# A mixture-of-experts block on one core: one-hots of seven batches made ahead by GpSimd, a ring of seven, logits copied by ScalarE

## The reference

```python
def _L0_ffn_ref(hidden_states, gate_w, Wg, Wu, Wd, Ws_g, Ws_u, Ws_d):
    b, s, d = hidden_states.shape            # 32, 256, 128
    e = gate_w.shape[0]                      # 16 experts
    cap = int(s * 2.0 / e)                   # 32 rows of each batch for each expert
    logits = jnp.einsum('bsd,ed->bse', hidden_states, gate_w)
    scores = jax.nn.softmax(logits, axis=-1).transpose(0, 2, 1)
    topk_w, topk_idx = jax.lax.top_k(scores, cap)
    x_tok = jnp.take_along_axis(hidden_states[:, None, :, :], topk_idx[..., None], axis=2)
    g = jnp.einsum('becd,efd->becf', x_tok, Wg)
    u = jnp.einsum('becd,efd->becf', x_tok, Wu)
    h = jax.nn.gelu(g, approximate=False) * u
    eo = jnp.einsum('becf,edf->becd', h, Wd) * topk_w[..., None]
    ...
    flat = flat.at[flat_idx].add(eo.reshape(-1, d))
    ...
    shared = jnp.einsum('bsf,df->bsd', jax.nn.gelu(gs, approximate=False) * us, Ws_d)
    return out + shared
x = L0_attn_x
x = x + _layernorm(_L0_attn_ref(_layernorm(x), ...))
x = x + _layernorm(_L0_ffn_ref(_layernorm(x), ...))
```

## Time and profile before

| | |
|---|---|
| median of 3 runs | 1394.62 us |
| lowest and highest | 1392.88 and 1401.41 us |
| profiled execution | 1400.59 us |
| its span, first to last instruction | 1398.9 us |
| TensorE busy | 1094.9 us, 78% of the span |
| VectorE busy | 1103.3 us, 79% |
| ScalarE busy | 889.4 us, 64% |
| GpSimd busy | 938.9 us, 67% |

### The profile page before, as it was taken

One profiled execution on the slowest core, in us unless ns is written; L12 is line 12 of the kernel. 1 busy time (PEld: TensorE's weight loads), 2 busy tenths in 40 slices (PEclk: granted clock), 3 DMA queues, 4 the chain that ended last, 5 costly groups with the idle time before them and its releaser, 6 DMA issues. The chain is left out here.

```text
span 1398.9 us, 15385 instructions
## 1 busy us (share of the span) xinstructions
PE 1094.9 (78%) x4128; PEld 510.1 (36%) x4128; DVE 1103.3 (79%) x1440; ACT 889.4 (64%) x1614; POOL 938.9 (67%) x503
## 2 busy tenths in 40 slices
PE   4667878787777878777777876445998989999796
PEld 2322222222222222222222322133755336666695
DVE  7499999999999999999999999896382962222288
ACT  3567577667667677667667665356332866666796
POOL 0199999999999999999999999722010740000176
PEclk9878899989999899989998898867798999999898
DMA  5745835834834835834834836110000001111013
GB/s 159 152 101 112 183 71 111 182 81 101 182 77 105 182 75 107 182 85 97 182 81 101 183 81 162 41 31 1 1 0 23 1 1 34 44 35 34 12 31 91
DMA packets 48490, 122.87 MB, mean 88 GB/s; under 512 B 5824, under 2 KB 20928, under 8 KB 42304
## 3 DMA queue, kind: packets, MB, share of 16 engines
q1 hardware_dynamic: 46864, 121.01, 39.1%
q10 hardware_dynamic: 1584, 1.36, 0.3%
HBM read 83.55 MB, written 5.24 MB: 63 GB/s over the span
## 5 line engine op out<-in xcount | busy, mean ns | idle before, releaser
L555 POOL TENSOR_TENSOR states<-b_dup,dup 128x1024 f32<-128x1024 f32 x256 | 596.5, 2359 | 63.3 <-DMA dup<-dd 61.7
L648 DVE TENSOR_TENSOR_SCAN da<-da,states 128x1024 f32<-128x1024 f32 x160 | 359.5, 2283 | 38.7 <-ACT da L397 32.6
L397 ACT ACTIVATE da<-dup,decay 128x510 f32<-128x510 f32 x512 | 327.2, 672 | 11.1 <-DVE states L648 11.1
L295 PE MATMUL yp<-states,fold 128*64 128x512 f32 x1024 | 275.4, 664 | 15.6 <-DVE states L574 9.8
L534 POOL TENSOR_TENSOR states<-states,X 128x1024 f32<-128x1024 f32 x96 | 226.1, 2356 | 20.5 <-DVE states L648 20.4
L648 DVE TENSOR_TENSOR_SCAN states<-da,states 128x1024 f32<-128x1024 f32 x96 | 218.7, 2278 | 7.0 <-ACT da L397 7.0
L574 DVE TENSOR_TENSOR states<-da,X 128x1024 f32<-128x1024 f32 x160 | 192.5, 1203 | 0.0
L1664 POOL TENSOR_SCALAR put<-row_t,slot_i,slot_w 128x256 f32<-128x256 f32 x32 | 39.1, 1222 | 193.3 <-POOLq L1368 173.5
L393 ACT ACTIVATE da<-zeros 128x4 f32<-128x4 f32 x177 | 30.5, 173 | 197.2 <-DVE states L574 196.3
L295 PEld LDWEIGHTS yp<-states,fold 128*64 128x64 f32 x1024 | 69.4, 152 | 212.5 <-issue 196.2
L1469 DVE TENSOR_TENSOR hx<-glx,upx 128x512 f32<-128x512 f32 x64 | 41.3, 684 | 126.6 <-ACT glx L1434 118.2
(11 more groups left out here) (185 smaller groups left out, 1779.9 us busy)
## 6 DMA issues: line engine op xcount, KB each, us to landing
b_dup<-bc_rows SPq DMA_DIRECT2D x32, 1024.0 KB, 9.6
dup<-dd SPq DMA_DIRECT2D x128, 256.0 KB, 11.7
X<-bc_rows SPq DMA_DIRECT2D x64, 512.0 KB, 11.5
out<-X SPq DMA_DIRECT2D x3, 1024.0 KB, 5.1
wg<-in_wgT SPq DMA_DIRECT2D x16, 128.0 KB, 2.1
wu<-in_wuT SPq DMA_DIRECT2D x16, 128.0 KB, 2.2
wd<-in_wdT SPq DMA_DIRECT2D x16, 128.0 KB, 2.2
bc_rows<-bcf SPq DMA_DIRECT2D x16, 64.0 KB, 1.6
```

The lines of the kernel that those rows point to most:

```text
L295: last = nc.tensor.matmul(yp[64 * i:64 * i + 64, :], fold[:], states[:, (2 * step + i) % RING, s, :], start=False, stop=(q == 3 and s == S ...
L397: ins = nc.scalar.activation(factors[:, s, :].rearrange("p (b t) -> p b t", b=2)[:, :, 1:S], src[:, :, 1:S], ACT.Exp, scale=decay[:, col:c ...
L555: nc.gpsimd.tensor_tensor(states[:, i % RING], b_dup[:, par, s0:s0 + SPI, :], dup[:, par, 1, h, g, :].unsqueeze(1).broadcast_to([P, SPI, N ...
L648: nc.vector.tensor_tensor_scan(to.rearrange("p s t -> p (s t)"), factors.rearrange("p s t -> p (s t)"), ring.rearrange("p s t -> p (s t)") ...
```

## The change

Two edits. First, the copy of the logits from `lp` to `L` moves from DVE to ACT; the first half is taken by ACT behind its copy of the turned pair 8, the second after its loop over the pairs. Second, `put` becomes a ring of seven batches (`PUTS`), allocated before the routed experts. During that block POOL makes all four one-hots of batches 0 to 6, 28 instructions. In the last stage PE waits for one-hots only from batch 7 on; DVE makes those of batch `n + 7` in `finish(n)`, POOL and ACT run ahead as far as the ring allows. With this go the places of the group steps: ACT's `inverse` stands at batches 14, 21 and 28, POOL's additions of the three groups begin at 17, 23 and 31, and DVE normalises three tiles in each of four batches of a group (the 4th to the 7th) where it had two in each of six.

```diff
+PUTS = 7
...
+                def take_logits(half):
+                    act.wait_ge(lp_ready, LP * (half + 1))
+                    nc.scalar.activation(L[:, CH * LP * half:CH * LP * (half + 1), :], lp[:].rearrange("p (c e) -> p c e", e=E),
+                                         ACT.Copy).then_inc(lp_free, 1)
...
+                    if n == LP:
+                        take_logits(0)
                     for s, q in SCALED_AT:
...
+                take_logits(1)
                 for m in range(EARLY, PAIRS):
                     gelu(m, 0)
...
-                    if n == LP + 1:
-                        take_logits(0)
...
-                take_logits(1)
                 dve.wait_ge(lp_free, 2)
...
+        put = sb("put", [P, PUTS, EG, S])
...
+        @block.gpsimd
+        def _(pool):
+            for n in range(PUTS):
+                for e in range(put.shape[2]):
+                    nc.gpsimd.tensor_scalar(put[:, n, e, :], row_t[:], slot_ib[:, e, n:n + 1], slot_wb[:, e, n:n + 1],
+                                            ALU.is_equal, ALU.mult).then_inc(put_first, 1)
+            pool.wait_ge(put_first, PUTS * put.shape[2])
...
+    NORM_ACT, ADD_POOL = (14, 21, 28), (17, 23, 31)
...
-                pe.wait_ge(put_dve, n + 1)
-                pe.wait_ge(put_pool, n + 1)
-                pe.wait_ge(put_act, n + 1)
+                if n >= PUTS:
+                    pe.wait_ge(put_dve, n - PUTS + 1)
+                    pe.wait_ge(put_pool, n - PUTS + 1)
+                    pe.wait_ge(put_act, n - PUTS + 1)
                 if n > 1:
                     pe.wait_ge(y_ready, n - 1)
...
-                if n > 1:
-                    act.wait_ge(yp_ready, n - 1)
+                act.wait_ge(yp_ready, n - PUTS + 1)
...
-            for n in range(B):
-                places(n)
-                g, i = (n - 11) // GB, (n - 11) % GB
-                if g >= 0:
-                    if i == 0:
+            for n in range(PUTS, B + 2):
+                if n < B:
+                    places(n)
+                for g, first in enumerate(NORM_ACT):
+                    if n == first:
                         inverse(g)
-                    elif 1 <= i < 1 + CHUNKS:
-                        norm(g, i - 1)
+                    elif first < n <= first + CHUNKS:
+                        norm(g, n - first - 1)
...
-                if n + 2 < B:
-                    places(n + 2)
+                if n + PUTS < B:
+                    places(n + PUTS)
...
-                    elif i >= 2:
-                        if i == 2:
+                    elif 3 <= i < 3 + CHUNKS:
+                        if i == 3:
                             offset(g)
-                        for t in mine[3 * CHUNKS * g + 2 * (i - 2):3 * CHUNKS * g + 2 * (i - 1)]:
+                        for t in tiles_of(g, i - 3)[0]:
                             norm(t)
...
-            for n in range(B):
-                places(n)
-                g, i = (n - 15) // GB, (n - 15) % GB
-                if g >= 0 and i < CHUNKS:
-                    add(g, i)
-            for i in range(B - 15 - GB * (G4 - 2), CHUNKS):
-                add(G4 - 2, i)
+            for n in range(PUTS, B + CHUNKS):
+                if n < B:
+                    places(n)
+                for g, first in enumerate(ADD_POOL):
+                    if first <= n < first + CHUNKS:
+                        add(g, n - first)
```

More of the change, by code:

```diff
@@ L1189, in experts @@
         first_out = sb("first_out", [P, 1, B, DM])
-        run_experts(nc, XG, XO, first_out, weights, w_in, load_weights)
-        scatter(nc, X, Y, [first_out[:, 0]] + [XO[:, g] for g in range(EG - 1)], row_t, slot_i, slot_w, eps, out_v, k)
+        put = sb("put", [P, PUTS, EG, S])
+        run_experts(nc, XG, XO, first_out, weights, w_in, load_weights, put, row_t, slot_i, slot_w)
+        scatter(nc, X, Y, [first_out[:, 0]] + [XO[:, g] for g in range(EG - 1)], put, row_t, slot_i, slot_w, eps, out_v, k)
 def by_two(eng, count, body, tail=1):
@@ L1355, in _, with run_experts @@
             pool.wait_ge(low_ready, B)
-def run_experts(nc, XG, XO, first_out, weights, w_in, load_weights):
+def run_experts(nc, XG, XO, first_out, weights, w_in, load_weights, put, row_t, slot_i, slot_w):
     E, B, CAP = XG.shape[1:]
@@ L1472, in _, with scatter @@
             dve.wait_ge(hx_ready, FH * 2 * E)
-def scatter(nc, X, Y, made, row_t, slot_i, slot_w, eps, out_v, k):
+def scatter(nc, X, Y, made, put, row_t, slot_i, slot_w, eps, out_v, k):
     S, DM, TILES = k["S"], k["DM"], k["TILES"]
@@ L1487, in sb @@
             return c.enter_context(nc.sbuf_tensor(name, shape, F32))
-        put = sb("put", [P, 2, EG, S])
         dist = sb("dist", [P, 2, AE, S])
@@ L1548, in places @@
                     nc.scalar.activation(dist[:, n % 2, e], row_t[:], ACT.Abs, bias=neg_i[:, e, n:n + 1]).then_inc(dist_ready, 1)
-                if n > 1:
-                    act.wait_ge(yp_ready, n - 1)
+                act.wait_ge(yp_ready, n - PUTS + 1)
                 for e in range(AE):
-                    act.wait_ge(dist_ready, AE * n + e + 1)
-                    ins = nc.scalar.activation(put[:, n % 2, ON_ACT + e], dist[:, n % 2, e], ACT.Relu,
+                    act.wait_ge(dist_ready, AE * (n - PUTS) + e + 1)
+                    ins = nc.scalar.activation(put[:, n % PUTS, ON_ACT + e], dist[:, n % 2, e], ACT.Relu,
                                                scale=neg_w[:, e, n:n + 1], bias=slot_wb[:, ON_ACT + e, n:n + 1])
@@ L1634, in add @@
                 nc.vector.tensor_tensor(xv, xv, chunk_of(Y, g, chunk), ALU.add).then_inc(x_dve, 1)
-            mine = [t for g in range(G4) for chunk in range(CHUNKS) for t in tiles_of(g, chunk)[0]]
-            places(0)
-            places(1)
             for n in range(B):
```

21 lines of the change are left out of this document (8 added, 13 removed).

## The result

The changed kernel took **1381.89 us** (median of 4 executions, 1381.34 to 1382.56), the kernel before 1393.75 in the same comparison (4 executions, 1392.64 to 1401.41): a ratio of 0.9907, 95% interval 0.9892 to 0.9922. The forecast was 1388.8, its range 1382.0 to 1395.5. The time went down by 11.9 us where 5.8 were forecast. The profiled execution of the changed kernel took 1381.92 us, its span is 1380.2. Most executions of the kernel before lie in two groups, near 1393 to 1397 and near 1401 to 1404; the one profiled in the earlier trace rows (1400.59) is of the later group, which the experiments explain in part.

The account below looks back on a forecast made before the run. PE was taken to bound the first block and the last stage's ordinary batches, DVE those with normalisations. Entry -3.6, tail -0.4 and first block -1.8 make -5.8 off the median 1394.62: 1388.8 us, range 1382 to 1395.5.

Parts of the forecast that it names:

- Entry, start: Entry of the last stage: PE needs no one-hot there and starts at about 1315.6 instead of 1319.21, 3.6 us earlier.
- Entry, clock: Entry of the last stage: PE's clock falls again in the pause and costs the same 5.7 us at half clock.
- the rival that had 0.12: Entry of the last stage: the clock doesn't fall in the shorter pause, giving 2.85 us back, 1385.9; chance 0.12.
- (b): Measured stretch of the trace, from ACT's table load at the last stage's entry to the 9th of 32 additions out of PSUM.
- Rhythm: Last stage, two full groups of eight batches: DVE's work decides, about 17.4 us a group, no gain, bounds -1.2 and +1.1.
- the 1 that the prediction named as a sign of being wrong: Last stage: the forecast is wrong if a group's period differs from 17.4 us by more than 1.
- First rival (one-hot not held): Last stage: POOL's addition doesn't hold DVE's one-hot, or only its start; group 15.2 us, -4.4, 1384.4; chance 0.17.
- Tail: End of the last stage: POOL's addition starts two instructions earlier against DVE's work, so the last variance is held less: 0.4 us.
- First block: First block of the expert part: with the logits copy on ACT, the down product of pair 2 starts 1.8 us earlier.
- One-hots in the experts: Routed experts: POOL's 28 one-hots, 34 us on an idle engine, cost DVE's work there 0; bound +1.
- The rival that POOL's one-hots hold DVE: Last stage, 12 batches with normalisations: each one-hot on POOL holds DVE 0.89 us longer, +4.9 in sum, 1399.5; chance 0.05.
- ACT's waits: Last stage: ACT's waits for variance and shift stand in front of later one-hots; priced 0 to +2 us, taken as 0.

Follow-up runs that it names:

- before: The kernel before the change, its first profile: the profiled execution took 1400.59 us; median 1393.75 us in the comparison with the changed kernel.
- before_again: The kernel before, unchanged, profiled once more: 1397.44 us over 12 executions, the profiled one 1393.35 us.
- ring_only: The changed kernel with the copy of the logits back on DVE: 1388.11 us, ratio 0.9954 to the kernel before.
- ring_only_again: The changed kernel with the copy of the logits back on DVE, profiled a second time: 1393.51 us over 12 executions.
- busy_entry: The kernel before with 8 extra products on PE at the entry of the last stage, ahead of its wait for one-hots: 1399.10 us, ratio 1.0017.
- busy_first_9: The kernel before with 9 extra products in PE's pause of the first block, ahead of the logits of pair 8: 1393.23 us, ratio 0.9956.
- busy_stats_7: The changed kernel with DVE's one-hot behind the statistics and 7 extra products in PE's first-block pause: 1382.45 us, ratio 0.9866 to the kernel before.
- logits_only: The kernel before with only the copy of the logits moved to ACT, two put buffers kept: 1392.95 us, ratio 0.9979.
- late_start: The changed kernel with PE's first product of the last stage made to wait for four extra ACT instructions: 1386.84 us.
- busy_first: The kernel before with 18 extra products in PE's pause of the first block, ahead of the logits of pair 8: 1398.38 us.
- after: The changed kernel, its first profile: median 1381.89 us, ratio 0.9907 to the kernel before; the profiled execution took 1381.92 us.
- after_again: The changed kernel, unchanged, profiled once more: 1380.57 us, ratio 0.9896 to the kernel before.
- stats_first: The changed kernel with DVE's one-hot behind the two statistics instead of ahead of them: 1381.24 us.
- no_addition: The changed kernel with POOL's additions of the first three groups replaced by a one-element-a-row instruction with the same waits: 1379.38 us.
- old_places: The changed kernel with the group steps of ACT, POOL and DVE at their places of before: 1383.01 us, ratio 0.9907 to the kernel before.
- ring_shift: The changed kernel with the logits copy on DVE and two extra products (1.3 us) for PE in the last expert: 1393.90 us.
- busy_stats: The changed kernel with DVE's one-hot behind the statistics and 14 extra products in PE's first-block pause: 1384.70 us.

## Why the prediction was wrong, and where it was right

- **Entry, start: right.** -3.6 forecast, 3.73 measured at the first product.
- **Entry, clock: the step that failed first.** "that fall lies before 1315.6, so I assume that it comes again and costs the same 5.7 us at half". It did not come; the rival that had 0.12 holds, with its 2.85 (2.7 measured as the rest of (b)). The step took the moment of the fall from one execution as a property of the pause, and counted the two edits apart where they worked together. The 17 profiles can be sorted by where PE stopped behind the last rise of its clock (at the gather; the rise read from the granted clock, the stop from the end of the last down product):

| PE stopped behind the last rise | profiles | the clock fell after PE stopped |
|---|---|---|
| 222.3 to 222.6 us | before, before_again, ring_only, ring_only_again, busy_entry, busy_first_9, busy_stats_7 | 2.6 to 2.9 us, inside the pause of each |
| 223.5 to 223.7 us, pause of 7.0 to 7.2 us | logits_only, late_start, busy_first | 5.0 to 5.2 us |
| 223.5 to 223.7 us, pause of 3.5 us | after, after_again, stats_first, no_addition, old_places | no fall: PE was back at 3.5 us |
| 223.9 to 224.1 us, pause of 3.5 us | ring_shift, busy_stats | 4.6 to 4.7 us, when PE was back for 1.0 to 1.2 us |

  So neither edit alone gave these 2.7 us: with the ring alone the fall came at 2.6 to 2.9 us, inside the short pause; with the copy alone it came at 5.2, inside the long one. Together the short pause ends before the later fall. The copy on ACT goes with the place and does not decide as such: in busy_first it is on DVE and the fall comes late, in busy_stats_7 it is on ACT and the fall comes early. That the distances repeat to 0.3 us within a kernel's profiles and sort all 17 is shown; that the place is the cause rests on this sorting and on the moved fall of ring_shift, not on a run that took the fall away by the place alone. The 2.7 us hang on a margin of a few tenths.
- **Rhythm: the second step that failed.** "That makes 16.8 to 17.9, in the middle 17.4: **no gain**". From the 14th to the 22nd addition the group took 16.27 (17.42 before), from the 22nd to the 30th 15.37 (17.36): both differ from 17.4 by more than the 1 that the prediction named as a sign of being wrong. The sum of work was nearly right: the held one-hot cost 0.82 (1.23 - 0.41), not 1.0, four times, which makes 16.1 of the 16.8. Wrong was to carry over the "waits of up to 1.1" of the kernel before, and to call the former waits for one-hots "off the path". With two buffers PE waited in each group for ACT's one-hots and for DVE's, and DVE in turn for PE; lines of the kernel before:

```profile
1363.24 0.46 PE L1539 MATMUL yss<-first_out,put 128*128 128x128 f32 x2 [0.37 <-ACT put L1553]
...
1365.31 0.42 DVE L1597 TENSOR_TENSOR xhT<-yss,xhT 128x256 f32<-128x256 f32 x1 [0.73 <-PE yss L1539]
...
1376.40 0.49 PE L1539 MATMUL yss<-first_out,put 128*128 128x128 f32 x2 [0.47 <-DVE put L1592]
```

  And in the four batches between, POOL made one one-hot and one addition a batch, without idle time, 2.43 us, and DVE's second normalisation, held, ended with POOL's addition; POOL alone:

```profile
1367.73 1.22 POOL L1664 TENSOR_SCALAR put<-row_t,slot_i,slot_w 128x256 f32<-128x256 f32 x1
1368.92 1.25 POOL L1671 TENSOR_TENSOR X<-X,xhT 128x512 f32<-128x512 f32 x1
1370.16 1.21 POOL L1664 TENSOR_SCALAR put<-row_t,slot_i,slot_w 128x256 f32<-128x256 f32 x1
```

  The ring lifts these ties: in the changed kernel all one-hots from ACT, DVE and POOL are ready 1.6 us or more before PE starts on them, up to the 30th batch. old_places, with the ring alone, gains 2.5 of the 3.0. From the 22nd to the 30th addition it gains more, since the batches with the last group's normalisations have no one-hot of DVE left to be held; the last one is made in the 25th batch. With the old places these eight batches took 16.24 all the same, since ACT was the bound. That POOL's cycle and these waits made the former period is read from the lines, and was not tested by itself; in stats_first, where POOL again has no idle time, the additions stand 2.49 apart in those batches, the length of POOL's cycle.
- **First rival (one-hot not held): false.** It is held for the rest of POOL's addition, as "near 1.3 us in place of 0.42" said.
- **Tail: right in kind, mis-sized.** 0.4 forecast, 1.3 measured: the variance is not held at all (0.17 for the 1.12 of the earlier trace rows), and the two normalisations that stood ahead of it (0.59 at 1387.86) now lie before the last addition.
- **First block: right.** 1.8 forecast, 1.9 measured at the down product, 2.1 to 2.4 by the entry. Not foreseen: the copy on ACT ends the late return of the clock, which 28 of 79 executions before had. Why the copy does so was not settled; with PE at work in the pause (busy_first) the group over 1400 goes too.
- **One-hots in the experts: right, 0.** The same 684 ns on DVE. The rival that POOL's one-hots hold DVE is false: three normalisations beside one take 0.91 (above), two took 0.58. The Trainium skill, "SBUF — State Buffer", section "Who interferes with whom", has a DVE instruction in a two-port mode and a GpSimd instruction exclude each other; the trace agrees for the additions (1.23 for 0.41) and not for the one-hots. No run shows in which mode DVE's one-hots and normalisations work.
- **ACT's waits: taken as 0, nearly right.** Up to the 30th batch PE waited for no one-hot of ACT; it waited four times for DVE's addition, 2.4 us in all. At the 31st and 32nd it starts 0.26 us after ACT's last one-hot, and these additions stand 2.07 and 2.17 apart in place of 1.79, 0.7 us in all; DVE, three normalisations a batch, had no idle time there either, so that no one engine can be charged with them. old_places shows what ACT's waits can cost when they come earlier. The 1.97 us a batch counts the overlap of neighbouring instructions twice: one after another, ACT's batches follow at 1.78 (the distances start at 1369.40 and 1371.18 in the kernel before), and at 2.17 with a normalisation.

Sum: -5.8 as forecast, -2.7 clock, -3.0 rhythm, -0.9 tail, -0.6 first block (2.4 for 1.8) and -0.1 start: -13.1 against an execution of before with early clock, 1381.5 from the median of 1394.62, where 1381.89 was measured. That base is luck: two of the three executions shown were of the early group, and with a median of the later group the time would have gone down by some 7 us more.

## What to carry to other kernels

Take no low-clock stretch of a single profile as a price: look at several executions, and put the clock into the range as an event of its own. Price two edits together where one moves the moment of an event and the other the pause that it falls into. When a ring loosens engines, work out each engine's own cycle in the batch, here POOL's one-hot and addition (2.43 us) and ACT's one-hots and normalisation (2.17), before waits of the old schedule are carried over. An addition on POOL that starts when DVE hands over its tiles should lie over DVE's reads of PSUM and its statistics, not over SBUF instructions of the held kind; then look which engine's cycle is next.

## What the runs showed of the hardware

- A pause of one length (3.5 us) met a fall of PE's clock (2.4 to 1.2 GHz) or none, and a fall also came 1.0 to 1.2 us after PE had resumed. In 12 of the 17 profiles the clock fell 2.6 to 5.2 us after PE had stopped; the 5 without a fall had PE back at 3.5 us.
- Behind a pause of 9.2 us the clock came back 4.4 us after PE resumed in one execution of the kernel before and 14.6 in another (4.4 to 4.8 or 14.5 to 14.6 over six profiles with this pause). Even behind a pause of 1.24 us (busy_first_9) the clock fell, 0.9 us after PE had resumed; behind one of 1.41 us (busy_stats_7) it did not.
- A float32 product of 512 columns is two matmul records of 0.43 us at full clock; three fillers were twice too long for it.
- POOL's addition of two SBUF tiles holds DVE's one-hot until it ends (1.23 for 0.41), and not DVE's addition out of PSUM (0.42) or its statistics (0.49 for two in stats_first), while POOL's one-hot holds neither DVE's one-hot nor its normalisations by an amount that shows (0.42, and 0.91 for three normalisations in the changed kernel).
